# Attention on one core: keys loaded and maximised by halves, another order of the unit's matmuls, GpSimd's five sums reordered

## The reference, cut to what matters

```
h = layernorm(x) * (1 + scale) + shift
q, k, v = h @ Wqkv + bqkv            # 16 heads of 32
attn = softmax(q k^T / sqrt(32))     # 1024 x 1024 for each head and batch
h = (attn @ v) @ Wproj + bproj
x = x + gate * h                     # then an MLP of width 2048, and the RMS norm
```

## Time and profile before

| | us |
|---|---|
| median of three runs | 3730.32 |
| the profiled execution, its own time | 3731.57 |
| its span, first to last instruction | 3729.7 |
| attention starts (first score) | 570.8 |
| attention's last loop ends (unit 63's first score) | 2235.7 |
| TensorE busy | 3689.7 (99%) |
| GpSimd busy in attention, 900 to 2200 us | 1210.6 of 1300 |
| VectorE busy there | 1167.2 of 1300 |
| ScalarE busy there | 897.2 of 1300 |

### The profile page before, as it was taken

One profiled execution on the slowest core, in us unless ns is written; L12 is line 12 of the kernel. 1 busy time (PEld: TensorE's weight loads), 2 busy tenths in 40 slices (PEclk: granted clock), 3 DMA queues, 4 the chain that ended last, 5 costly groups with the idle time before them and its releaser, 6 DMA issues.

```text
span 3729.7 us, 50080 instructions
## 1 busy us (share of the span) xinstructions
PE 3689.7 (99%) x18430; PEld 2637.2 (71%) x18430; DVE 2444.4 (66%) x4107; ACT 1816.7 (49%) x3276; POOL 1957.8 (52%) x636
## 2 busy tenths in 40 slices
PE   8999999999999999999999999999999999999998
PEld 6788875455656565656556556888888888888887
DVE  6677668888988989889898983333443333434442
ACT  3222225666767676767676665333333333333333
POOL 1000116999999999999999996322231222222221
PEclk9999999999999999999999999999999999999999
DMA  8787776767776777677776764111111111111110
GB/s 285 246 270 241 244 246 137 154 143 164 164 171 150 164 160 174 151 157 162 171 160 151 165 147 143 43 44 61 46 37 46 37 46 37 46 37 46 37 46 23
DMA packets 219249, 480.41 MB, mean 129 GB/s; under 512 B 22931, under 2 KB 61843, under 8 KB 202755
## 3 DMA queue, kind: packets, MB, share of 16 engines
q1 hardware_dynamic: 200860, 345.08, 33.0%
q0 software_dynamic: 18144, 132.13, 17.2%
HBM read 225.36 MB, written 117.60 MB: 92 GB/s over the span
## 4 chain that ended last, share of the span: by engine, by line
PE 93%; POOL 3%; DVE 1%; issue 1%; ACT 1%; DMA 0%; SPq 0%; POOLq 0%; DVEq 0%; ACTq 0%
PE psum L736 12%; PE psum L1299 12%; PE psum L1313 12%; PE psum L595 10%; PE psum L597 10%; PE psum L596 10%; PE psum L1978 6%; PE psum L1974 6%; PE psum L1976 6%; PE psum L1344 4%; POOL probs_round L1578 2%; PE psum L1327 2%; PE psum L1927 1%; ACT probs L1445 0%; PE psum L745 0%
## 5 line engine op out<-in xcount | busy, mean ns | idle before, releaser
L1118 DVE TENSOR_REDUCE max_part<-psum 128x1 f32<-128x512 f32 x2048 | 1269.8, 679 | 68.4 <-PE psum L736 68.0
L1578 POOL TENSOR_TENSOR probs_round<-probs_round,probs_round 128x2048 f32<-128x2048 f32 x189 | 887.3, 4695 | 104.6 <-PE psum L1313 88.5
L2143 DVE TENSOR_TENSOR g_parts<-g_full,g_parts 128x512 fp32r<-128x512 f32 x256 | 259.3, 1013 | 805.5 <-ACT g_parts L2032 805.5
L1299 PE MATMUL psum<-q_stack,k_stack 128*128 128x512 f32 x2048 | 767.1, 400 | 0.8 <-ACT probs L1445 0.5
L736 PE MATMUL psum<-k_stack,q_stack 128*128 128x512 f32 x2048 | 755.0, 399 | 0.6
L1445 ACT ACTIVATE probs_round<-psum 128x512 f32<-128x512 f32 x1024 | 539.0, 603 | 329.8 <-PE psum L1299 327.1
L1445 ACT ACTIVATE probs<-psum 128x512 f32<-128x512 f32 x1024 | 544.0, 605 | 219.0 <-PE psum L1299 204.5
L1578 POOL TENSOR_TENSOR probs_round<-probs_round,probs 128x2048 f32<-128x2048 f32 x124 | 571.5, 4609 | 9.7
L2028 ACT ACTIVATE g_full<-psum,cols 128x512 f32<-128x512 f32 x256 | 176.6, 690 | 800.8 <-PE psum L597 800.4
L2239 POOL TENSOR_TENSOR y_out<-y_out,rows 128x512 f32<-128x512 f32 x60 | 77.3, 1288 | 853.0 <-DVE y_out L2178 853.0
L736 PEld LDWEIGHTS psum<-k_stack,q_stack 128*128 128x128 f32 x2048 | 383.8, 188 | 187.8 <-DVE max_part L1118 113.4
(11 more groups left out here) (193 smaller groups left out, 4949.9 us busy)
## 6 DMA issues: line engine op xcount, KB each, us to landing
probs<-probs POOLq DMA_DIRECT2D x126, 1024.0 KB, 7.7
qk_parts<-qk_out SPq DMA_DIRECT2D x128, 512.0 KB, 4.4
k_stack<-qk_parts SPq DMA_DIRECT2D x96, 512.0 KB, 7.0
q_stack<-qk_parts SPq DMA_DIRECT2D x192, 256.0 KB, 5.7
v_rows<-v_out SPq DMA_DIRECT2D x64, 256.0 KB, 3.8
v_group<-v_rows SPq DMA_DIRECT2D x32, 512.0 KB, 10.2
gated_attention<-gated SPq DMA_DIRECT2D x64, 256.0 KB, 4.7
x<-in_x SPq DMA_DIRECT2D x16, 1024.0 KB, 10.0
```

Source lines behind the costliest of these rows:

```text
L1118: dve.reduce_max(max_part[:, n:n + 1], psum[:, TURNS[at.turn][0], :], AX.X).then_inc(dve_smax, 1)
L1299: pe.matmul(psum[:, ST[n % 3], :], k_stack[G % 2][0:P, h, kt * P:(kt + 1) * P], q_stack[u % 3][0:P, h, :], start=True, stop=True).then_inc ...
L1578: pool.tensor_tensor(total[:, :, :], total[:, :, :], probs(u, kt)[:, :, :], ALU.add).then_inc(pool_sum, 1)
```

## The change

Keys: a group's keys are loaded in two halves of 512 tokens, three DMAs of 256 KB each. The first half of group G + 2 is loaded in odd loops, when the first 16 scores of the unit are done, and the second half of group G + 1 at the start of even loops, behind the queries. Maxima: first all 16 of the first half of the keys, then the 16 of the second half; each goes to the column of `max_part` that it had. `ORDER` is new: the first `V V` stands alone as before, the next stands one score ahead of `!` (`alVVs!`), and the last four around `D` (`VVDtrpnVV`); there are 10 `m` ahead of `!` where there were 18. `POOL_ORDER`: the add of tile 1 is now the first of a unit (1, 5, 3, 6, 7), and pair `B` is issued once tile 3's values step is done, which is now the `V` right before `D`.

```diff
 
 
 
-    ORDER = ("sgsmmmssmsmaVlVsmsswmmsmsmmVVmsmssmmsmmsmssVV!s"
-             "msmsmsmsmstrmspDVVmjmsjjjnmsmsjsmsjjsmsmjsmjjjj")
-
-
-
-    POOL_ORDER = "-1-3-6A-7B5"
+    ORDER = ("gsmssmmsmVVmwsmmsmssmmalVVs!smsmjssmmsjmssjmsmj"
+             "smsmsmsjsmsjmsmsmjsjmmVVDtrpnVVsmssmjmjsmsmjsmj")
+
+
+
+    POOL_ORDER = "-3-6A-7B15"
     LAST = KT - 1
     LEAD = N_MAX - ORDER.split("!")[0].count("m")
     PV_LAG = 2
@@ -289,7 +289,8 @@
         act_ahi, pool_alo, pe_proj2, dve_gated = (sem("act_ahi"), sem("pool_alo"),
                                                   sem("pe_proj2"), sem("dve_gated"))
         act_hicopy, dve_alo = sem("act_hi_copy"), sem("dve_alo")
-        a_k, a_q, a_m, a_vg = sems("a_k", 2), sems("a_q", 3), sems("a_m", 3), sems("a_vg", 2)
+        a_k = [sems(f"a_k{half}_", 2) for half in range(NCH)]
+        a_q, a_m, a_vg = sems("a_q", 3), sems("a_m", 3), sems("a_vg", 2)
         a_z = sems("a_z", 3)
         a_gated, a_g = sems("a_gated", 2), sems("a_g", 2)
         a_pair = {"A": sem("a_pair01"), "B": sem("a_pair23")}
@@ -436,7 +437,8 @@
                     if c == NC - 1 and j == 1:
                         sp.wait_ge(dve_centred, (NC - 1) * KD)
                         sp.wait_ge(dve_norm1, 4 * NC)
-                        load_keys(sp, 1)
+                        load_keys(sp, 1, 0)
+                        load_keys(sp, 1, 1)
                     elif c == NC - 1 and j == 4:
                         load_q(sp, 2)
                     sp_side(sp, side_load(side_step(c, j)))
@@ -524,9 +526,11 @@
                 sp.wait_ge(a_rows, 48)
                 for i in range(3):
                     sp.wait_ge(a_qk[i], 16 * ((2 * 2 * KD + 2 - i) // 3))
-                load_keys(sp, 0, (0,))
+                load_keys(sp, 0, 0, (0,))
+                load_keys(sp, 0, 1, (0,))
             elif (c, j) in ((NC - 4, 3), (NC - 4, 5)):
-                load_keys(sp, 0, (j // 2,))
+                load_keys(sp, 0, 0, (j // 2,))
+                load_keys(sp, 0, 1, (j // 2,))
             elif c == NC - 3 and j in (1, 5):
                 load_q(sp, j // 5)
             elif (c, j) == (NC - 2, 1):
@@ -537,15 +541,16 @@
                 sp.dma_start(probs_own[0][:, :, :],
                              t["Wproj"].rearrange("(k p) n -> p k n", p=P)).then_inc(a_wproj, 16)
 
-        def load_keys(sp, G, parts=(0, 1, 2)):
+        def load_keys(sp, G, half, parts=(0, 1, 2)):
             b, g = divmod(G, NG)
             at = D + g * P
+            cut = slice(half * CH, (half + 1) * CH)
             for n in parts:
                 part = n % 2
                 sp.dma_start(
-                    k_stack[G % 2][n * HD:(n + 1) * HD, :, :].bitcast(fp32),
-                    qk_dram[b, part, at:at + P, :].rearrange("(h d) t -> d h t", h=GH)
-                ).then_inc(a_k[G % 2], 16)
+                    k_stack[G % 2][n * HD:(n + 1) * HD, :, cut].bitcast(fp32),
+                    qk_dram[b, part, at:at + P, cut].rearrange("(h d) t -> d h t", h=GH)
+                ).then_inc(a_k[half][G % 2], 16)
 
         def load_values(sp, G):
             b, g = divmod(G, NG)
@@ -714,14 +719,18 @@
         LAST_DEN, *LEFT_BANKS = [bank for bank in (*SMAX, SPARE) if bank != TAIL_DEN]
         LEFT_BANKS.append(TAIL_DEN)
 
+        def max_place(n):
+
+            kh, rest = divmod(n, GH * TT)
+            return kh, *divmod(rest, TT)
+
         def pe_maximum(pe, at):
             u, n = divmod(at.n, N_MAX)
             if u >= NU:
                 return
             at.n += 1
             G = u // NCH
-            h, rest = divmod(n, TT * NCH)
-            i, kh = divmod(rest, NCH)
+            kh, h, i = max_place(n)
             if n == 0:
                 pe.wait_ge(a_q[u % 3], 48 * (u // 3 + 1))
                 if u >= 3:
@@ -729,7 +738,8 @@
                 else:
                     pe.wait_ge(pool_zero, (2, 3, 5)[u])
                     pe.wait_ge(pool_ones, min(G, 1) + 1)
-                pe.wait_ge(a_k[G % 2], 48 * (G // 2 + 1))
+            if h == 0 and i == 0:
+                pe.wait_ge(a_k[kh][G % 2], 48 * (G // 2 + 1))
             bank, freed, count = TURNS[at.turn]
             if count > 0:
                 pe.wait_ge(freed, count)
@@ -1115,7 +1125,9 @@
             dve.wait_ge(pe_smax, at.turn + 1)
             if n == 0 and u:
                 dve.wait_ge(dve_gather, u)
-            dve.reduce_max(max_part[:, n:n + 1], psum[:, TURNS[at.turn][0], :],
+            kh, h, i = max_place(n)
+            column = (h * TT + i) * NCH + kh
+            dve.reduce_max(max_part[:, column:column + 1], psum[:, TURNS[at.turn][0], :],
                            AX.X).then_inc(dve_smax, 1)
             at.turn += 1
             if n == N_MAX - 1:
@@ -1245,20 +1257,25 @@
                 G, half = divmod(u, NCH)
                 b = u // PER_B
                 tile = u - PROJ_LAG
-                if half == 0 and 0 < u and G + 1 < NGRP:
-                    sp.wait_ge(pe_st, u * 32)
-                    sp.wait_ge(pe_smax, ring_of_send(u - 1) + 1)
-                    load_keys(sp, G + 1)
                 if 0 < u and u + 2 < NU:
                     sp.wait_ge(pe_st, u * 32)
                     load_q(sp, u + 2)
+                if half == 0 and 0 < u and G + 1 < NGRP:
+                    sp.wait_ge(pe_smax, ring_of_send(u - 1) + 1)
+                    load_keys(sp, G + 1, 1)
                 if u % PER_B == 2 and b:
                     if b >= 2:
                         sp.wait_ge(dve_gated, 8 * (b - 1))
                     load_gates(sp, b)
-                values = 0
+                scores = values = 0
                 for what in ORDER:
-                    if what == "!":
+                    if what == "s":
+                        scores += 1
+                        if scores == N_MAX // 2 + 1 and half == 1 and G + 2 < NGRP:
+                            sp.wait_ge(pe_st, u * 32 + N_MAX // 2)
+                            sp.wait_ge(pe_smax, ring_of_send(u) + 1)
+                            load_keys(sp, G + 2, 0)
+                    elif what == "!":
                         send_max(sp, u + 1)
                         if u == NU - 2:
                             load_first_chunk(sp)
```

## The result

The changed kernel takes 3741.75 us, the median of nine runs (3739.55 to 3743.78); the kernel before, run beside it, 3731.75 (3730.3 to 3734.2). The ratio is 1.0027, with a 95% interval of 1.0016 to 1.0037: slower by 10 us, or 0.27%. The profiled execution has a span of 3740.4 us and took 3742.14; its granted clock is 0.999, as before.

A forecast was written before the change was run, and what follows sets the result against it. TensorE's own row (26.52 us a loop) bounds attention, with GpSimd's cycle of sums close at 26.29. Loops -4.5, start +6.2, end -2.3 sum to -0.6 us: 3731.0 profiled, 3729.7 median, no change; range 3720 to 3749.

The forecast's parts named there:

- the rival of the late A: Odd loops: half of the keys goes ahead of pair A, deciding from 8.2 us landing (26.59 a loop); 3748 us, chance 0.25.
- Three runs, turn between full matmuls: TensorE's loop: three runs of values steps for four gain 0.33 us; `!` between full matmuls costs 0.10.
- TensorE's own loop: TensorE's own instruction row per attention loop: 26.52 us becomes 26.29, with ends 26.19 to 26.52.
- A's landing, 7.9 us in odd loops: Pair A beside the half of the keys lands 7.9 us after its issue, with ends 6.9 and 9.2.
- two loops take 44.97 + L, if that is more than 52.58: GpSimd's cycle, L being A's landing time in odd loops: 7.9 gives 52.87 for two loops, 26.44 a loop.
- Even loops free: In even loops the load shrinks by 0.75 MB, so pair A finds the queue empty and lands after 6.9 us.
- Ring 26.29: GpSimd's cycle from `D` through tile 4's values step and five adds to the next `D` stays 26.29 us.
- Loops 1 to 8 at nothing: In the first eight loops GpSimd's cycle of sums already binds, so nothing is won there.
- Start +6.2, end -2.3: Attention starts 6.2 us late behind more early maxima; the last loop wins 2.3 with fewer scores and products behind `D`.
- Costs taken as nothing: SyncE's extra wait and issues, VectorE's reduces and bank turns in loops cost nothing; at most 0.1 us a loop for banks.
- The rival with the taking of turns: Late A in odd loops through DMA engines alternating between queues packet by packet; 3748 us, chance 0.25.
- the strict one: Strict taking of turns: pair A loses the full 2.3 us, lands at 9.2, and the sum is 34 us more.

The follow-up runs named there:

- the ring is shortened: Changed kernel with tile 5 added over two of its four heads only, shortening GpSimd's cycle of sums: 3712.08 us (one run).
- A earlier: Changed kernel with pair A issued one add earlier, behind tile 3's add instead of tile 6's: 3726.14 us, ratio 0.9984 to the kernel before.
- halves alone: Changed kernel with ORDER and POOL_ORDER of the kernel before, leaving only keys and maxima by halves: 3734.93 us, ratio 1.0011 to the kernel before.
- two thirds of the half: Changed kernel with two of the half's three key loads in odd loops, the third at the even loop's start: 3732.50 us, ratio 1.0007 to before.

## Why the prediction was wrong, step by step

The forecast, 3729.7 us and no change, was 12 us too low (1.4 of them because the kernel before ran that much slower beside the changed one); the time is inside the range and on the slower side. The forecast and the rival of the late A have one mechanism, the half of the keys ahead of A, and differ in its price. The mean distance of `D` came out as 26.59, exactly where that rival begins, but not by its landing: the median is 7.8, not 8.2 or 8.6. What was mis-sized is the sum over the single landings.

- **Three runs, turn between full matmuls: right.** 4.48 us and 0.11 us in the trace, 26.28 for TensorE's own loop where the ring is shortened (26.31 without the short last one).
- **A's landing, 7.9 us in odd loops: right in the mean, wrong as a single value.** Its mean is 7.92, its median 7.80. The step that failed is the one that put one L into "two loops take 44.97 + L, if that is more than 52.58". Every landing above 7.6 is paid in full and none below it is paid back, and five of 26 odd loops have landings of 8.5 to 9.6. Over the 27 odd loops from 9 to 61 the first add is late by 0.44 us on average where 0.29 was worked out: 27 x 0.15 = 4.0 us. 0.07 of the 0.15 is the time from landing to add, 0.17 and not the 0.1 that I took without a row for it. The trace of the kernel before already had such a spread: beside loads, in even loops, A landed after 7.1 to 10.0 us.
- **Even loops free: wrong.** A lands at 6.86 there, as taken, but at 8.1 in loop 18 and 9.1 in loop 28, with no load beside it (in loop 28 the values had landed 3 us before its issue); in loop 56 the add is 0.5 late with A in time. 26 loops times 0.10: 2.7 us.
- **Ring 26.29:** the undisturbed distance is 26.31, another 1.1 us. TensorE's own row (26.31 in the kernel with the shorter ring) and GpSimd's ring (24.2 from the add to the next `D`, and 2.09) are too close to tell which of them sets it. These three make 7.8 of the 8.2 us by which the 53 loops were missed.
- **Loops 1 to 8 at nothing: wrong, +2.2.** I said only that nothing is won where the ring binds. A's landing enters the ring there too: in loops 6 and 7 it lands at 9.0 and 8.4. With A earlier the stretch is 210.2 again.
- **Start +6.2, end -2.3: right.** +6.9 and -2.2; 0.8 of the first is stage 1's own (the product above), which leaves 6.1. At the end GpSimd's wait for ScalarE, 2.49 us in the earlier trace rows, has become

```profile
2249.08 1.29 POOL L1571 TENSOR_TENSOR attn_lo<-attn_other,attn_hi 128x512 fp32r<-128x512 f32 x1 [0.43 <-ACT attn_hi L1407]
```

- **Costs taken as nothing** (bank turns, VectorE, SyncE's new waits): right but for a little. For VectorE's maxima TensorE waits once, 0.7 us at the start of attention. For ScalarE its scores wait six times in the whole execution, 3.5 us, of which one wait of 0.6 lies in loops 9 to 62. Loading by halves was not free in the orders of before: about 3 us, by way of pair B.
- **The rival with the taking of turns.** A lost 0.9 us beside key bytes of which, by the forecast's working, 2.3 us were still open, so the price is less than half of the strict one. Where the half was issued right behind A (halves alone), both sides lost: A 2.1 us, and the keys landed 8.8 to 10.2 us after their issue instead of the 3.1 to 4.6 of loop 47 in the changed kernel. The Trainium skill (DMA: Bandwidth & Descriptors, Queues, rings and completion order) has the engines take turns between queues packet by packet. The losses on both sides are in line with it; no run here shows in what shares.

## What to carry to other kernels

A transfer that is put into a ring with no slack costs its spread, not its mean: sum the part of each landing that exceeds the slack, and ask first whether it can be issued earlier. Here one letter of GpSimd's order, moved one add ahead, turned 10 us slower into 6 us faster, since the new order of TensorE had made room for it. The same letter in the old order cost 230 us, part of it by TensorE's clock: a wait of 2.4 us in each loop also costs what the clock loses behind it, so look at the granted clock of a loop before you price its wait. And a load taken out of one consumer's way goes into another's: list who is queued behind it at its new place before moving it.

## What was not expected of the hardware

- The late landings of A are no chance: they recur in the same loops in several kernels (13, 18, 23, 49 and 59). They go with packets of instruction fetches on the same DMA engines, which the trace shows as queues of their own (instruction, one packet of 0.3 to 2.1 us). In the kernel with two thirds of the half, A lands at 6.9 us on average and 7.5 at most in the 41 loops (9 to 61) that have no such packet in flight between 0.3 and 6 us after its issue, and at 7.7 on average, 9.1 at most, in the 12 that have one. In the changed kernel the odd loops without one have a mean of 7.61 and at most 8.15, the seven with one 8.67. Loop 28's 9.1 has none, and no run here moved a fetch, so it goes along with them and isn't shown to be caused by them. The queues in the first 6 us of A's flight (packets, MB, share of 16 engines), changed kernel, loop 49 and, behind the dots, loop 43:

```profile
q0 software_dynamic: 99, 0.81, 64.4%
q1 hardware_dynamic: 326, 0.58, 41.7%
q8 instruction: 1, 0.02, 1.4%
...
q0 software_dynamic: 105, 0.86, 68.0%
q1 hardware_dynamic: 299, 0.53, 41.4%
```

  Half a megabyte of keys is in both; only loop 49, where A lands at 9.6, has the instruction packet.
- Small copies suffer more than large ones. In loop 43 of the halves alone, the two 8 KB copies of the maxima, issued beside A and the keys, took 8.0 and 8.4 us; in the changed kernel they take 2.2 and 2.3 in that loop, 1.8 in the median.
- Beginnings differ: the same products of stage 1 start up to 2 us apart between the profiled executions. Each kernel has one trace, so whether it goes by kernel or by execution is open. A difference at the start of attention has to be read against a product ahead of it.
